# Moving POOL's power for the next tile between the second and the third scatter of the merged stage

## The chip, the cores and the metric

The kernel runs on one core of one Trainium2 chip. The metric is the device time of one execution in microseconds, as the median of several runs. Engines: TensorE (PE), VectorE (DVE), ScalarE (ACT), GpSimd (POOL), and SyncE (SP), which issues plain DMAs.

## The reference

The input has 8,192 tokens of 128 features in fp32. Three blocks follow each other, each with a layer norm ahead and a residual add behind: half of a mixture of experts, linear attention, and half of the same mixture of experts again.

```python
x = x + 0.5 * ffn(layernorm(x), ...)      # mixture of experts
x = x + attention(layernorm(x), ...)      # 32 sequences of 256 tokens, 16 heads of 8
x = x + 0.5 * ffn(layernorm(x), ...)      # mixture of experts, same weights

# ffn: a shared expert for every token, and 2 of 8 routed experts, inner size 256
shared = (silu(x @ shared_gate.T) * (x @ shared_up.T)) @ shared_down.T
probs = sigmoid(x @ router_w.T + routing_bias)
scores, indices = top_k(probs, 2);  scores = scores / sum(scores)
combined = sum over the two picks of score * expert(x)
return shared + combined

# attention: phi = silu + 1, no softmax
kv = phi(k)^T v per head;  out = phi(q) kv;  return out @ Wo.T + bo
```

## The kernel before

Tokens are handled in 16 tiles of 512 (four sub-tiles of 128). There are four stages.

1. **Dispatch** (`f = 0`): each tile is normalised, routed and run through the shared expert. POOL scatters its rows (input, two weights, two addresses) by indirect DMA into regions of DRAM by expert, `first_rows`.
2. **Slots** (`f = 0`): 78 slots of 256 rows go through the routed experts, once for the first picks and once for the second. POOL scatters the results.
3. **Merged stage** (366 to 592 us in the profile): attention and the dispatch of the second mixture of experts run interleaved, one tile of each per turn. In turn `i` attention works on tile `i`, the projections of tile `i + 1`, the transposes and the routing of tile `i - 1` (`LAG_T = 1`) and the shared expert of tile `i - 2` (`LAG_G = 2`).
4. **Slots** (`f = 1`), and the output.

Each engine has its own list of instructions, written out by hand in the order of its turns; the engines meet at semaphores only. An engine that waits holds up everything behind it in its list.

What matters for the change are the steps of the merged stage that hand work from one engine to another, by the tile that they belong to:

- VectorE, turn `i`: `mask_heads(i)` (`kv_sb`), `add_bias(i)`, `value(i + 1, 0)` (`v_sb`), in turns 0 to 8 a late pick (`add_pick`, `x<-xT_lo,x`), the second half of the routing of tile `i - 2` (`place` and four short steps), `multiply(.., 0)` (`h`), `low` (`xT_lo`), `value(i + 1, 1)`, statistics for the late pick or, in later turns, three steps of `first_table`, `add_attention(i)`, `norm_stats` and `variance` (`var`) of tile `i`, the first 13 routing steps of tile `i - 1` (each some 0.22 us from start to start, the last writes `mask`), `shift_rows` (`shift`) of tile `i`, in some turns a `normaliser` of ten steps for a group of up to four attention tiles, `multiply(.., 1)` (`h`), three more routing steps and the reciprocal, `add_shared`.
- POOL, tile `t = i - 2` in turn `i`: `row_numbers`, `pick_weights` (it waits for `place` of its tile; five instructions that end with the write of the weights into `send`), four indirect scatters, and then `deviation`, which is the power: it takes the -0.5th power of `var` of tile `t + 2` and writes `rstd`.
- ScalarE: `send_normalised(1, i)` (`send`) needs `shift` and `rstd` of tile `i`; `high` (`xT_hi`) copies the transposed tile, and VectorE's `low` needs that copy.
- TensorE: the gate and up products of the shared expert (`g_bank`, `u_bank`, lines 1015 to 1017) in two halves, `times_wo` (L1271), transposes (L1037), projections (L1248, L1254), `attend` (L1280), `router` (L1058, it needs `xT_lo`), `down_shared` (L1101), `key_value` (L1264), `ranks` (L1070). The first half of the gate products of a turn needs VectorE's second `h` of the turn before.

`variance(q)` raises `norm_step`, for which `deviation(q)` waits; `deviation` raises `rstd_done`, for which `shift_rows` waits. The power of tile 1 stands ahead of POOL's tile loop, those of tiles 2 to 15 inside it. `norm_step` and `rstd_done` count in the same order before and after.

Of the kernel before, what the change touches and what calls it, by code (L numbers as in the profile page):

```python
# [42 lines left out]
FFN, ATTN = "ffn", "attention"  # L43
LAG_T, LAG_G = 1, 2
# [22 lines left out]
NORM_OF = {item: (q, i) for q, items in enumerate(NORMS) for i, item in enumerate(items)}  # L67
# [7 lines left out]
LOGITS_READ, MASK_STEP, SAFE_STEP, RECIP_STEP, RANKS_READ = 2, 13, 16, 17, 19  # L75
PLACES_STEP = 20
NORM_STEPS, POWER_STEPS = 10, 2
POWER_AFTER = 4
NORM_AHEAD = {4: NORM_OF[(FFN, 0, 8)][0], 8: NORM_OF[(FFN, 0, 12)][0]}
POWERS = list(NORM_AHEAD.values()) + [NORM_OF[(FFN, 1, t)][0] for t in range(NEWTON, TILES)]  # L80
STEPS_OF = [POWER_STEPS if q in POWERS else NORM_STEPS for q in range(len(NORMS))]
# [36 lines left out]
def macaron(nc, x_in, w_experts, router_wT, routing_bias, w_attn, bq, bv, bo, out):  # L118
    tokens = x_in.shape[0]
    tiles = TILES  # L120
# [18 lines left out]
    with ExitStack() as ctx:  # L139
# [217 lines left out]
        def ring_of(f, t):  # L357
            return (f * tiles + t) % SEND_RING
# [37 lines left out]
        def batch_no(f, b):  # L396
            return f * len(BATCHES[0]) + b
# [221 lines left out]
        def _(pool):  # L619
# [36 lines left out]
            def deviation(q):  # L656
                n = len(NORMS[q]) * SUB
                pool.wait_ge(norm_step, STEPS_BEFORE[q] + 1)
                for kind, f, s in NORMS[q - 2]:
                    if kind == FFN:  # L660
                        pool.wait_ge(send_xn_done, f * tiles + s + 1)
                pool.tensor_tensor(rstd[q % 2][:, 0:n], var[:, 0:n], neg_half[:, 0:n], ALU.pow).then_inc(rstd_done, 1)  # L662

            def row_numbers(f, t):
                if f == 0 and t == 0:
                    pool.wait_ge(numbers_ready, 1)
                wait_count(pool, sent[ring_of(f, t)], sent_count(f, t - SEND_RING))
                pool.tensor_copy(send[ring_of(f, t)][:, :, NUMBER].bitcast(I32), number[:, t * SUB:(t + 1) * SUB]
                                 ).then_inc(row_numbered, 1)

            def ffn_tile(f, t):
                b = BATCH_OF[f][t]
                i = t - BATCHES[f][b][0]
                row_numbers(f, t)
                if f == 1:
                    pick_weights(t)
                    pool.wait_ge(weights_step, WEIGHT_STEPS * (t + 1))
                pool.wait_ge(route_step, (batch_no(f, b) + 1) * ROUTE_STEPS)
                pool.wait_ge(row_numbered, f * tiles + t + 1)
                pool.wait_ge(send_xn_done, f * tiles + t + 1)  # L680
                for j in range(SUB):
                    k = i * SUB + j
                    pool.indirect_dma_start(  # L683
                        first_rows, bass.IndirectOffsetOnAxis(ap=send_to[b % SEND_TO_RING][:, k:k + 1], axis=0),
                        send[ring_of(f, t)][:, j, :], None).then_inc(sent[ring_of(f, t)], 16)
                if f == 1 and t + LAG_G < tiles:
                    deviation(NORM_OF[(FFN, 1, t + LAG_G)][0])

            def pick_weights(t):
                n = SUB  # L690
                picks = [a[:, :, 0:n] for a in (score_silu, score_recip, prob)]
                pool.wait_ge(score_silu_done, batch_no(1, t) + 1)
                pool.wait_ge(route_step, batch_no(1, t) * ROUTE_STEPS + RECIP_STEP + 1)
                pool.tensor_tensor(picks[2], picks[0], picks[1], ALU.mult).then_inc(weights_step, 1)
                pool.wait_ge(weights_step, WEIGHT_STEPS * t + 1)
                pool.tensor_tensor(total[:, 0:n], prob[:, 0, 0:n], prob[:, 1, 0:n], ALU.add).then_inc(weights_step, 1)
                pool.wait_ge(weights_step, WEIGHT_STEPS * t + 2)
                pool.tensor_scalar(total[:, 0:n], total[:, 0:n], 2.0, None, ALU.mult).then_inc(weights_step, 1)
                pool.wait_ge(weights_step, WEIGHT_STEPS * t + 3)
                pool.tensor_tensor(inv_total[:, 0:n], total[:, 0:n], minus_one[:], ALU.pow).then_inc(weights_step, 1)  # L700
                pool.wait_ge(weights_step, WEIGHT_STEPS * t + 4)
                wait_count(pool, sent[ring_of(1, t)], sent_count(1, t - SEND_RING))
                pool.tensor_tensor(send[ring_of(1, t)][:, :, WEIGHT:WEIGHT + PICKS].rearrange("p s w -> p w s"), picks[2],
                                   inv_total[:, 0:n].unsqueeze(1).to_broadcast([P, PICKS, n]), ALU.mult).then_inc(weights_step, 1)
# [16 lines left out]
            def dispatch():  # L721
                f = 0
                ffn_tile(f, 0)
                ffn_tile(f, 1)
                split_low(1)
                ffn_tile(f, 2)
                ffn_tile(f, 3)
                split_low(2)
                split_low(3)
                for ts in BATCHES[f][WRITTEN_OUT:]:  # L730
                    for t in ts:
                        ffn_tile(f, t)
                        q = NORM_AHEAD.get(t)
                        if q is not None:
                            deviation(q)
                    for t in ts:
                        if 1 <= t < EXPERTS:
                            split_low(t)
# [1383 lines left out]
```

## Time and profile before

| | us |
|---|---|
| median of 3 runs | 810.29 |
| lowest, highest | 806.66, 812.32 |
| profiled execution, its own time | 810.85 |
| its span | 809.1 |
| TensorE busy | 704.3 (87%) |
| VectorE busy | 553.4 (68%) |
| ScalarE busy | 461.8 (57%) |
| POOL busy | 485.5 (60%) |

Shares of busy time are means over stages that have different limits. TensorE's granted clock was 0.938 of full speed over the span. The time of the execution is 1.75 us longer than the span: what lies around the first and the last recorded instruction.

### The profile page before, as it was taken

Reading aid. Unit: us, or ns where it says so; the run is one execution under the profiler, and the core shown is the slowest. Engines: PE = TensorE matmul, PEld = TensorE weight load, DVE = VectorE, ACT = ScalarE, POOL = GpSimd, SP = SyncE. Lnnn points to the kernel's source line nnn. Section 1 sums busy time; section 2 is a strip of 40 time slices with the busy share of each in tenths; the row PEclk is TensorE's granted clock in tenths of the full one; section 3 lists DMA queues with packets and bytes.
Section 4 is the critical chain, followed back from the end, with each engine's and each line's share of the span. In section 5 each row is a group of like instructions: output and inputs, shape, how many; then the busy total and the mean of one; then the engine's idle time right before and its main releaser. Section 6 shows DMA issues by size and latency. Waiting matters only on the chain.

```text
span 809.1 us, 18241 instructions
## 1 busy us (share of the span) xinstructions
PE 704.3 (87%) x5229; PEld 652.7 (81%) x5229; DVE 553.4 (68%) x1730; ACT 461.8 (57%) x849; POOL 485.5 (60%) x580
## 2 busy tenths in 40 slices
PE   5578849979999899998888989998779999899990
PEld 4466748869999899996677778887679999899990
DVE  6688697875455556787887877787675555455673
ACT  2334525347667657767665657754247667657760
POOL 5253655647777677773354454555537777667773
PEclk7589989989999999999899999999799999999996
DMA  9111163127787475641120000000326788466676
GB/s 279 60 46 45 57 178 89 54 82 207 213 235 242 138 209 169 192 125 34 40 60 21 15 28 15 28 21 22 88 68 192 207 237 233 158 190 180 187 233 230
DMA packets 87956, 103.27 MB, mean 128 GB/s; under 512 B 12212, under 2 KB 70452, under 8 KB 87860
## 3 DMA queue, kind: packets, MB, share of 16 engines
q1 hardware_dynamic: 72244, 64.97, 30.1%
q0 software_dynamic: 15616, 37.14, 12.8%
q8 instruction: 46, 0.75, 0.4%
q14 instruction: 50, 0.41, 0.2%
HBM read 51.57 MB, written 50.49 MB: 126 GB/s over the span
## 4 chain that ended last, share of the span: by engine, by line
PE 42%; POOL 18%; DVE 13%; issue 9%; DMA 3%; ACT 3%; SPq 1%; POOLq 0%; DVEq 0%; ACTq 0%
PE y_bank L1207 11%; POOL first_rows L683 6%; POOL second_rows L712 6%; PE g_bank L1015 4%; PE g_bank L1017 3%; PE g_bank L1016 3%; PE u_bank L1015 3%; PE u_bank L1016 3%; PE u_bank L1017 3%; PE y_bank L1101 3%; DMA row_ring<-second_rows 2%; POOL rstd L662 2%; POOL inv_total L700 2%; DVE h L1439 2%; PE route_bank L1161 1%
## 5 line engine op out<-in xcount | busy, mean ns | idle before, releaser
L1877 DVE TENSOR_TENSOR h<-silu_g,u_bank 128x512 f32<-128x512 f32 x144 | 99.0, 688 | 145.1 <-ACT silu_g L894 138.8
L712 POOL DMA_INDIRECT second_rows<-row_ring x144 | 138.9, 965 | 65.1 <-issue 41.7
L683 POOL DMA_INDIRECT first_rows<-send,send_to x128 | 126.4, 988 | 85.8 <-DVE send L1540 41.6
L712 POOL DMA_INDIRECT y_rows<-row_ring x144 | 141.9, 986 | 58.2 <-issue 32.7
L869 ACT ACTIVATE slot_gu<-w_gu 128x1024 fp32r x132 | 139.8, 1059 | 42.4 <-issue 42.2
L1207 PE MATMUL y_bank<-w_dn,h 128*128 x1152 | 153.1, 276 | 0.2 <-DVE h L1877 0.2
L1207 PEld LDWEIGHTS y_bank<-w_dn,h 128*128 128x128 f32 x1152 | 141.3, 192 | 0.9 <-issue 0.4
L1015 PE MATMUL g_bank<-xT_hi,slot_gu 128*128 128x256 f32 x264 | 86.5, 328 | 12.8 <-DVE xT_lo L1868 12.7
L894 ACT ACTIVATE silu_g<-g_bank 128x512 f32<-128x512 f32 x144 | 83.8, 582 | 15.5 <-PE g_bank L1017 15.3
L1101 PEld LDWEIGHTS y_bank<-w_dn,h 128*128 128x128 f32 x512 | 66.1, 204 | 17.8 <-issue 15.7
L1101 PE MATMUL y_bank<-w_dn,h 128*128 128x128 f32 x512 | 67.3, 288 | 13.5 <-DVE x L1444 13.5
L797 ACT ACTIVATE send<-x,shift,rstd 128x128 f32<-128x128 f32 x128 | 52.2, 482 | 44.6 <-DVE shift L1422 37.1
L1016 PE MATMUL u_bank<-xT_lo,slot_gu 128*128 128x256 f32 x264 | 75.1, 285 | 0.0
L1017 PE MATMUL g_bank<-xT_hi,slot_gu 128*128 128x256 f32 x264 | 75.1, 284 | 0.0
L1017 PE MATMUL u_bank<-xT_hi,slot_gu 128*128 128x256 f32 x264 | 74.9, 284 | 0.0
L1016 PE MATMUL g_bank<-xT_lo,slot_gu 128*128 128x256 f32 x264 | 74.9, 284 | 0.0
L1015 PE MATMUL u_bank<-xT_hi,slot_gu 128*128 128x256 f32 x264 | 74.9, 284 | 0.0
L788 ACT ACTIVATE silu_g<-g_bank 128x512 f32<-128x512 f32 x64 | 38.1, 595 | 60.2 <-PE u_bank L1017 60.0
L1015 PEld LDWEIGHTS g_bank<-xT_hi,slot_gu 128*128 128x128 f32 x264 | 50.6, 192 | 15.0 <-DVE xT_lo L1868 14.6
L1016 PEld LDWEIGHTS g_bank<-xT_lo,slot_gu 128*128 128x128 f32 x264 | 50.9, 193 | 0.0
L1016 PEld LDWEIGHTS u_bank<-xT_lo,slot_gu 128*128 128x128 f32 x264 | 50.5, 191 | 0.0
L1017 PEld LDWEIGHTS g_bank<-xT_hi,slot_gu 128*128 128x128 f32 x264 | 50.5, 191 | 0.0
(257 smaller groups left out, 1638.2 us busy)
## 6 DMA issues: line engine op xcount, KB each, us to landing
row_ring<-second_rows SPq DMA_DIRECT2D x66, 258.0 KB
row_ring<-first_rows SPq DMA_DIRECT2D x66, 132.0 KB
w_raw<-w_experts SPq DMA_DIRECT2D x21, 256.0 KB, 2.8
second_rows<-pad SPq DMA_DIRECT2D x16, 258.0 KB
x<-x_in SPq DMA_DIRECT2D x16, 256.0 KB, 7.1
xT_hi<-y_rows SPq DMA_DIRECT2D x16, 256.0 KB
xT_lo<-y_rows SPq DMA_DIRECT2D x16, 256.0 KB, 2.9
out<-x SPq DMA_DIRECT2D x16, 256.0 KB
```

The costliest lines, as they stand in the source:

```text
L683: pool.indirect_dma_start(first_rows, bass.IndirectOffsetOnAxis(ap=send_to[b % SEND_TO_RING][:, k:k + 1], axis=0), send[ring_of(f, t)][:, ...
L712: pool.indirect_dma_start(to, bass.IndirectOffsetOnAxis(ap=rows[k][:, j, at:at + 1].bitcast(I32), axis=0), rows[k][:, j, columns], None).t ...
L788: act.activation(silu_g[c][:], g_bank[gate_bank(n, c)][:], ACT.Silu).then_inc(silu_done, 1)
L797: last = act.activation(send[ring_of(f, t)][:, j, INPUT:RESULT], x_sub(t, j), ACT.Identity, bias=bias, scale=scale)
L869: act.activation(slot_gu[n % 2][:].rearrange("p a n -> p (a n)"), w_gu[:, bass.ds(e, 1)].rearrange("p e a n -> p (e a n)").bitcast(F32), A ...
L894: act.activation(silu_g[n % 2][:], g_bank[n % 2][:], ACT.Silu).then_inc(slot_silu_done, 1)
L1015: pe.matmul(bank_ap, w_parts[0], x_parts[0], start=True, stop=False)
L1016: pe.matmul(bank_ap, w_parts[0], x_parts[1], start=False, stop=False)
L1017: return pe.matmul(bank_ap, w_parts[1], x_parts[0], start=False, stop=True)
L1101: last = pe.matmul(shared_bank[:, s], h[t % 2][c][:, s], w_dn[:, 0, c, :], start=(c == 0), stop=(c == HALVES - 1))
L1207: last = pe.matmul(y_bank[par][:, j * P:(j + 1) * P], h[par][0][:, c * ROWS + j * P:c * ROWS + (j + 1) * P], w_dn[:, bass.ds(e[j % len(e)] ...
L1877: dve.tensor_tensor(h[par][0][:], silu_g[par][:], u_bank[par][:], ALU.mult).then_inc(slot_h_done, 1)
```

## The change

The call of `deviation` for tile `t + LAG_G` moves from behind the loop over the four scatters into it, behind the second scatter. Its arguments, its waits and its semaphore stay the same, and so do all other engines' lists. The constant `POWER_AFTER` is not used by the kernel before. Tiles 14 and 15 have no such call.

```diff
-POWER_AFTER = 4
+POWER_AFTER = 2
...
                 for j in range(SUB):
                     k = i * SUB + j
                     pool.indirect_dma_start(
                         first_rows, bass.IndirectOffsetOnAxis(ap=send_to[b % SEND_TO_RING][:, k:k + 1], axis=0),
                         send[ring_of(f, t)][:, j, :], None).then_inc(sent[ring_of(f, t)], 16)
-                if f == 1 and t + LAG_G < tiles:
-                    deviation(NORM_OF[(FFN, 1, t + LAG_G)][0])
+                    if f == 1 and j + 1 == POWER_AFTER and t + LAG_G < tiles:
+                        deviation(NORM_OF[(FFN, 1, t + LAG_G)][0])
```

## Rows read from the trace of the kernel before

**Rows 1.** Waits from 366 to 592 us: waiter, releaser, total, times, longest.

```profile
DVE shift L1422 <- POOL rstd L662: 21.3, 14, 2.2
```

**Rows 2.** Timeline of POOL in turn 10: start, us, operation, idle before it.

```profile
518.82 0.96 POOL L683 DMA_INDIRECT first_rows<-send,send_to  x1 [0.30 <-issue]
...
521.34 0.95 POOL L683 DMA_INDIRECT first_rows<-send,send_to  x1 [0.30 <-issue]
522.31 1.06 POOL L662 TENSOR_TENSOR rstd<-var,neg_half 128x4 f32<-128x4 f32 x1
...
526.99 0.20 POOL L694 TENSOR_TENSOR prob<-score_silu,score_recip 128x8 f32<-128x8 f32 x1 [3.48 <-DVE place L1518]
```

**Rows 3.** Timeline of DVE in the same turn.

```profile
514.23 0.22 DVE L1518 TENSOR_TENSOR place<-route_bank,filled 128x64 f32<-128x64 f32 x1
...
518.83 0.18 DVE L1414 TENSOR_SCALAR var<-stats 128x4 f32<-128x4 f32 x1
...
521.61 0.19 DVE L1500 TENSOR_TENSOR mask<-best,first_best 128x32 bf16<-128x32 f32 x1
523.40 0.16 DVE L1422 SCALAR_TENSOR_TENSOR shift<-stats,rstd 128x4 f32<-128x4 f32 x1 [1.60 <-POOL rstd L662]
```

**Rows 4.** Timeline of PE in the same turn.

```profile
511.83 0.50 PE L1015 MATMUL g_bank<-xT_hi,w_gu 128*128 128x512 f32 x1 [0.24 <-DVE h L1439]
...
515.29 1.05 PE L1280 MATMUL y_bank<-kvo_sb,phi_q 128*128 128x128 f32 x8
516.47 0.28 PE L1058 MATMUL route_bank<-router_parts,xT_hi 128*128 128x16 f32 x1
...
521.51 1.06 PE L1264 MATMUL y_bank<-phi_k,v_sb 128*128 128x128 f32 x8
522.40 0.60 PE L1037 MATMUL tr_bank<-ident,xn 128*128 128x128 f32 x4
...
524.22 0.50 PE L1015 MATMUL g_bank<-xT_hi,w_gu 128*128 128x512 f32 x1 [0.23 <-DVE h L1439]
```

**Rows 5.** Windows, power to power: PE, PEld, DVE, ACT, POOL busy; PE clock; DMA.

```profile
442.83:455.86 13.03, 12.06 (x82) 10.17 (x81) 10.72 (x38) 8.56 (x19) 7.08 (x11) 1.00 0.06 22
...
481.88:497.52 15.64, 13.43 (x82) 11.52 (x81) 11.21 (x45) 9.97 (x23) 7.06 (x11) 0.89 0.06 19
...
509.93:522.31 12.38, 12.01 (x82) 10.12 (x81) 10.04 (x38) 8.56 (x19) 7.06 (x11) 1.00 0.07 23
...
547.13:559.54 12.41, 11.60 (x78) 9.71 (x77) 10.17 (x38) 6.65 (x14) 7.06 (x11) 1.00 0.07 24
559.54:571.63 12.09, 8.91 (x65) 7.26 (x63) 9.36 (x36) 3.93 (x9) 7.12 (x12) 1.00 0.07 22
```

**Rows 6.** Timeline of DVE: shift behind the powers of four other turns.

```profile
414.05 0.16 DVE L1422 SCALAR_TENSOR_TENSOR shift<-stats,rstd 128x4 f32<-128x4 f32 x1 [1.59 <-POOL rstd L662]
...
427.66 0.16 DVE L1422 SCALAR_TENSOR_TENSOR shift<-stats,rstd 128x4 f32<-128x4 f32 x1 [0.95 <-POOL rstd L662]
...
560.62 0.16 DVE L1422 SCALAR_TENSOR_TENSOR shift<-stats,rstd 128x4 f32<-128x4 f32 x1 [1.48 <-POOL rstd L662]
...
572.71 0.16 DVE L1422 SCALAR_TENSOR_TENSOR shift<-stats,rstd 128x4 f32<-128x4 f32 x1 [1.98 <-POOL rstd L662]
```

**Rows 7.** Timeline of all engines round the first power in the tile loop.

```profile
398.40 1.06 POOL L662 TENSOR_TENSOR rstd<-var,neg_half 128x4 f32<-128x4 f32 x1
...
398.69 0.19 DVE L1500 TENSOR_TENSOR mask<-best,first_best 128x32 bf16<-128x32 f32 x1
...
399.49 0.16 DVE L1422 SCALAR_TENSOR_TENSOR shift<-stats,rstd 128x4 f32<-128x4 f32 x1 [0.61 <-POOL rstd L662]
```

**Rows 8.** Timeline of all engines, turn with a normaliser for four tiles.

```profile
482.96 0.16 DVE L1422 SCALAR_TENSOR_TENSOR shift<-stats,rstd 128x4 f32<-128x4 f32 x1 [1.61 <-POOL rstd L662]
...
485.12 1.65 ACT L781 ACTIVATE xn<-x,attn_shift,attn_rstd 128x128 f32<-128x128 f32 x4 [5.06 <-DVE attn_shift L1406]
...
491.67 0.28 PE L1058 MATMUL route_bank<-router_parts,xT_hi 128*128 128x16 f32 x1
```

## The prediction

> **What bounds the kernel now.** I began with the table of waits over the merged stage (366 to 592 us) and looked for VectorE behind the operation that moves. VectorE's `shift` waited 14 times for POOL's power, 21.3 us together [rows 1]. The reader should ask whether this wait ends last, so next comes one turn on three engines. On POOL the scatters of a tile follow each other at 1.26 us, the power starts 0.02 us behind the end of the fourth (522.29) and ends at 523.37; then POOL is idle 3.48 us until the next tile's `place` [rows 2]. On VectorE `var`, which the power reads, is there at 519.01, the last mask of the routing ends at 521.80, and `shift` starts at 523.40: 1.60 us idle [rows 3]. Behind `shift` stand `h`, the bias, `v_sb` and the next `place`, and `place` starts POOL's next chain. So today's loop is place, POOL's weights, four scatters, power, shift, place. From `place` at 514.23 to the end of the power it takes 9.14 us.
>
> TensorE must be read with care. It is shown busy 12.01 of 12.38 us in a turn without a late pick, and 12.06 of 13.03 in one with it [rows 5]: the same work in more time. Its ends are modelled, so part of a wait is hidden in busy time. In the turn of [rows 4] it waits 0.24 us for `h` at 511.83. From the attention product (515.29) to the router (516.47) it takes 1.18 us, while eight matmuls of the same form elsewhere in the turn, from 521.51 to 522.40, take 0.89: another 0.29 us, spent waiting for `xT_lo`. TensorE's own turn is then 524.22 - 511.83 = 12.39, less 0.53: about 11.85 us.
>
> **The change part by part.** Nothing is added or removed; 14 powers move ahead of the third and fourth scatter of their tile. The power of the merged stage that stands before the tile loop does not move (it is the one I leave out: POOL waited for `var` there, not VectorE for POOL).
>
> *The power earlier.* The second scatter ends at 518.82 + 0.96 = 519.78, and `var` is ready at 519.01, 0.77 us before. The power ends at about 519.80 + 1.06 = 520.86, while VectorE reaches `shift` at 521.80. The wait is gone, with 0.94 us to spare. Should the power start 0.30 us behind a scatter, as the next scatter does [rows 2], it still hides. Bounds of what the move takes off VectorE in this turn: 1.60 us (all) and 0.
>
> *Two scatters later.* Scatters three and four end 1.06 us later, or 1.36 with another 0.30 us gap, by 523.65. POOL's row numbers (0.18) follow and POOL is then idle for over 3 us [rows 2]. The cover is 3.48 us long now; with a turn 0.55 us shorter and POOL free at 523.65 + 0.18, some 2.6 us of it are left (526.99 - 0.55 - 523.83). What reads those rows is a load far behind the tile's own turn. The `send` buffers are used again after six tiles. Cost 0. Without the cover it would be 0.3 us a tile.
>
> *The new wait of POOL.* If `var` came late, scatters three and four would wait behind it. It has 0.77 us in hand, and if the whole of `var`'s delay beyond that were real, the power would still end no later than it does now, so no loss can come from this side while `place` keeps its lead. I take 0; for each us by which `var` came later than that, scatters three and four would lose one, out of the 2.6 us of cover.
>
> *What is late next.* VectorE's own turn is 12.39 - 1.60 = 10.8 us here, and 13.03 - 1.6 = 11.4 with a late pick. TensorE needs 11.85 in both. So TensorE becomes the bound, and the saving is not the wait: **0.55 us in a turn of 12.39 and 1.17 in one of 13.03**. I count from one gate product on TensorE to the next:
> - Tile 0 (wait 0.61 us [rows 7]): 0. TensorE and ScalarE are behind there at half clock, and `h` would wait for `silu_g` instead.
> - Tiles 1 and 2 (1.59 and 0.95 [rows 6]): these turns carry two late picks, four extra statistics and the normaliser for four tiles, and VectorE bounds them: 2.5 us.
> - The turn behind them (ends at 444.7) is held by ScalarE's chain, then by TensorE: 0.2.
> - Two turns of 13.03: 2 x 1.17 = 2.3.
> - The pair from 470.8 to 499.4, one window like the first of [rows 5] and the one of 15.64 us there, 28.7 together. A normaliser of four tiles stands behind the shift. In the new frame, with the gate product at 0, the router starts at 516.47 - 511.83 - 0.29 = 4.35 and the mask ends 5.33 us later (521.80 - 516.47), at 9.7. From shift to `xn` takes 485.12 - 482.96 = 2.16, from `xn` to the router 491.67 - 485.12 = 6.55 [rows 8], and from router to the next gate product 11.85 - 4.35 = 7.5. Sum 25.9; saved 2.8.
> - Three turns of 12.39: 3 x 0.55 = 1.65, taken as 1.7.
> - The last three turns. In the first the transposes of the attention input are gone, TensorE is busy 0.41 us less (11.60 against 12.01 [rows 5]), bound 11.45, saved 1.0. In the other two TensorE has less still (8.91 us in the last window [rows 5]) and VectorE bounds: their waits of 1.48 and 1.98 [rows 6] go whole, 3.5.
>
> Sum: 2.5 + 0.2 + 2.3 + 2.8 + 1.7 + 4.5 = **14.0 us** of 21.3. The expert slots behind start that much sooner and are otherwise the same.
>
> *A rule against the change.* Until now VectorE stood idle for most of each power; now it routes beside it. In [rows 7] a power ran from 398.40 to 399.46 beside a mask step with two operands in SBUF: 0.19 us, as in [rows 3]. I count no contention. The Trainium skill, "SBUF — State Buffer", section "SBUF: two separate sides", says that a VectorE instruction with two SBUF inputs and a GpSimd instruction that reads SBUF lock each other out of a shared port for a whole instruction. By that rule the routing would stand still during the power; the row speaks against it, one case as it is. The second rival below is that case.
>
> **How the numbers follow.** The profiled execution took 810.85 us, 809.1 of them span. 810.85 - 14.0 = 796.9. It stands 0.56 us above the median of 810.29, so I forecast **796.3 us**. Runs of before lie between 806.66 and 812.32; about 1% (8 us) is what a measurement of this kernel can tell from no change.
>
> - **TensorE becomes the bound** (forecast): 0.60. Own range 793 to 800, from 0.2 us per turn either way in the 11.85.
> - **VectorE keeps all of its wait.** If the 11.85 is too long because the modelled matmuls hide more waiting, the whole 21.3 less the 0.61 of tile 0 comes back: 789.6. For it: the turn at 481.88 had its clock at 0.89 [rows 5], and fewer gaps may spare that. Against it: TensorE's matmuls start without a gap in the rest of the turn. Chance 0.10.
> - **Power and routing exclude each other.** VectorE stands still 1.06 us of the 1.60 it wins, its turns become 11.9 and 12.5 us, and each of 13 powers gives 0.54: 7 us, 803.3. The same figure stands for any latency that I took as covered (`xT_lo` has only some 0.1 us behind ScalarE's `xT_hi` in the new frame). Chance 0.17.
> - **The change does not do what it says**: the power would be held until the scatters' descriptors are finished, so that its end stays where it was. The gap of 0.02 us behind the fourth scatter [rows 2] speaks against it. 810. Chance 0.06.
> - **Slower: TensorE's clock.** It was granted at 1.00 (2.4 GHz) in the steady turns and 0.89 on average, so partly at 1.2 GHz, in the turn with the long gap [rows 5]. New, short waits in another place of each turn could bring it down each time. In the turn of 15.64 us TensorE's busy time is 1.4 us over the 12.01 of a steady one [rows 5]. At that price the gain of 14.0 is used up when 10 of 13 turns fall; in all 13 it costs 18 us, so 814.5. The steady turns hold 1.00 with gaps of 0.24 and more in TensorE, which speaks against it. Chance 0.03.
> - The remaining 0.04 is spread on either side.
>
> The range from the second case to the third, 789.5 to 803.5, leaves out about 0.15. Faster by over 1% (below 802.2) holds the first two, a third of the third and half of the remainder: 0.80. Within 1%: 0.17. Slower: 0.03.
>
> **What the changed profile would show.** The power stands between scatters two and three and ends about 1 us before `shift`; the row `shift` waits for `rstd` is gone or below 1 us in all; scatters three and four end about 1.1 to 1.4 us later against `place`; steady windows are 11.8 to 11.9 us with and without a late pick alike; VectorE now waits for ScalarE's `xT_hi` or `silu_g`, some 0.5 to 1 us a turn; mask steps keep 0.19 us. The forecast is wrong if turns with and without a pick still differ by 0.6 us (VectorE bounds, second rival or third), if the routing steps are stretched beside the power, or if the clock of a steady window falls below 1.00.

## The result and the profile after

| | before | after |
|---|---|---|
| median, us | 811.25 (4 runs) | 788.89 (4 runs) |
| lowest to highest, us | 806.66 to 812.32 | 786.57 to 789.84 |
| span of the profiled execution, us | 809.1 | 788.1 |

The ratio is 0.9731, with a 95% interval from 0.9686 to 0.9775: 2.7% faster, 22.4 us between the medians, 21.0 us between the spans. I had forecast 14.0 us and 796.3 us in all; the time lies 0.6 us under the range.

The page of the changed kernel: the span, each engine's busy time and the granted clock of TensorE in 40 slices.

```profile
span 788.1 us, 18241 instructions
...
PE 691.0 (88%) x5229; PEld 644.4 (82%) x5229; DVE 554.2 (70%) x1730; ACT 460.1 (58%) x849; POOL 486.5 (62%) x580
...
PEclk8588898989999999999999999999989999999995
```

The waits of the merged stage after the change (columns as in [rows 1]). The row of `shift` behind the power, 21.3 us before, is gone. POOL itself now waits for `var`: 9.6 of the 10.5 us belong to the power ahead of the tile loop, 0.33 and 0.54 to two tiles.

```profile
POOL rstd L662 <- DVE var L1414: 10.5, 3, 9.6
```

POOL and VectorE of the changed kernel in the turn of [rows 2] and [rows 3].

```profile
505.55 1.11 POOL L683 DMA_INDIRECT first_rows<-send,send_to  x1 [0.60 <-POOL send L703]
506.96 0.96 POOL L683 DMA_INDIRECT first_rows<-send,send_to  x1 [0.30 <-issue]
507.95 1.05 POOL L662 TENSOR_TENSOR rstd<-var,neg_half 128x4 f32<-128x4 f32 x1
509.19 1.03 POOL L683 DMA_INDIRECT first_rows<-send,send_to  x1 [0.20 <-issue]
```

```profile
502.38 0.21 DVE L1518 TENSOR_TENSOR place<-route_bank,filled 128x64 f32<-128x64 f32 x1
...
504.18 0.69 DVE L1433 TENSOR_TENSOR xT_lo<-tr_bank,xT_hi 128x512 fp32r<-128x512 f32 x1 [0.19 <-ACT xT_hi L770]
...
507.33 0.17 DVE L1414 TENSOR_SCALAR var<-stats 128x4 f32<-128x4 f32 x1
...
508.07 0.19 DVE L1493 TENSOR_TENSOR best<-z,score 128x32 f32<-128x32 f32 x1
508.30 0.19 DVE L1496 TENSOR_TENSOR best<-best,counting 128x32 f32<-128x32 f32 x1
...
510.10 0.19 DVE L1500 TENSOR_TENSOR mask<-best,first_best 128x32 bf16<-128x32 f32 x1
510.21 0.15 DVE L1422 SCALAR_TENSOR_TENSOR shift<-stats,rstd 128x4 f32<-128x4 f32 x1
```

The power starts 0.03 us behind the second scatter and ends at 509.00. The last mask step ends at 510.29 and `shift` starts at 510.21, with no wait. VectorE does wait for ScalarE's `xT_hi` (0.19 us): it has run ahead of the others. `shift` now starts 2.17 us ahead of the next first gate product (512.38), before the change 0.82 (523.40 and 524.22). Routing steps beside the power, at 508.07 and 508.30, read two operands in SBUF each and keep 0.19 us and a distance of 0.23. Behind the power the third scatter starts after 0.19 us and lasts 1.03 us instead of 0.96, and POOL's copy behind the fourth starts 4.54 us after the second scatter, before the change 4.52. The three windows below, again from power to power with the columns of [rows 5], are a turn with a late pick, one with the normaliser for four tiles, and one without a late pick.

```profile
437.33:448.71 11.38, 11.38 (x81) 10.08 (x80) 10.68 (x38) 8.46 (x20) 7.20 (x12) 1.00 0.07 24
...
471.42:485.54 14.12, 12.28 (x81) 10.23 (x80) 11.80 (x49) 8.38 (x20) 7.18 (x11) 1.00 0.07 21
...
496.54:507.95 11.41, 11.41 (x81) 10.10 (x80) 10.39 (x41) 8.57 (x20) 7.18 (x12) 1.00 0.08 25
```

Turns with and without a pick now have the same length, 11.4 us, and TensorE's busy time is the whole window. This is what the forecast said of the bound, at another size. One of its signs missed: it wanted VectorE to wait 0.5 to 1 us a turn. In the three turns without a pick VectorE waits 1.3 us together, and in the two with one it doesn't wait at all, so there its list is as full as TensorE's.

TensorE in the same turn of the changed kernel, then those lines of the kernel before that [rows 4] left out.

```profile
500.98 0.49 PE L1015 MATMUL g_bank<-xT_hi,w_gu 128*128 128x512 f32 x1
...
502.24 0.39 PE L1017 MATMUL u_bank<-xT_hi,w_gu 128*128 128x512 f32 x1
502.47 0.60 PE L1271 MATMUL y_bank<-attn_raw,kv_sb 128*128 128x128 f32 x4
502.91 0.60 PE L1037 MATMUL tr_bank<-ident,send 128*128 128x128 f32 x4
...
504.21 1.05 PE L1280 MATMUL y_bank<-kvo_sb,phi_q 128*128 128x128 f32 x8
505.02 0.26 PE L1058 MATMUL route_bank<-router_parts,xT_hi 128*128 128x16 f32 x1
...
512.27 0.25 PE L1072 MATMUL route_bank<-mask,all_ones 128*128 128x64 bf16 x4
512.38 0.49 PE L1015 MATMUL g_bank<-xT_hi,w_gu 128*128 128x512 f32 x1
```

```profile
513.09 0.39 PE L1017 MATMUL u_bank<-xT_hi,w_gu 128*128 128x512 f32 x1
513.44 0.71 PE L1271 MATMUL y_bank<-attn_raw,kv_sb 128*128 128x128 f32 x4
513.99 0.60 PE L1037 MATMUL tr_bank<-ident,send 128*128 128x128 f32 x4
...
523.74 0.25 PE L1072 MATMUL route_bank<-mask,all_ones 128*128 128x64 bf16 x4
```

The reader should compare starts with starts, not busy times. `u_bank` to `kv_sb`'s product: 0.35 us before, 0.23 after. That product to the transposes: 0.55 and 0.44. `attend` to the router: 1.18 and 0.81 (with its first step 0.03 more). Ranks to the next gate product: 0.48 and 0.11. Together 0.12 + 0.11 + 0.37 + 0.03 + 0.37 = 1.00 us, and the turn went from 12.39 to 11.40. I had found 0.53 of it.

From gate product to gate product (`g_bank`, L1015, the first half of each turn) the time divides so:

| stretch (times of the kernel before) | before | after | saved | forecast |
|---|---|---|---|---|
| 386.6 to 430.5: tiles 0, 1, 2 | 43.9 | 40.5 | 3.4 | 2.5 |
| to 444.7: the turn behind | 14.3 | 13.9 | 0.4 | 0.2 |
| to 470.8: two turns with a late pick | 26.0 | 22.8 | 3.3 | 2.3 |
| to 499.4: the pair with the normaliser | 28.7 | 25.5 | 3.2 | 2.8 |
| to 536.6: three turns without a pick | 37.2 | 34.2 | 3.0 | 1.7 |
| to 573.5: the last three with a power | 36.9 | 31.1 | 5.8 | 4.5 |
| to 595.4: last tiles, table, first slot | 21.9 | 18.3 | 3.6 | 0 |

The rows sum to 22.7; the first gate product came 0.4 us later and the slots behind took 214.9 us instead of 213.7, which leaves the 21.0 of the spans.

Two parts of this sum can't be laid to the change on these traces. One is the last row, which is taken up with the runs below. The other is 1.6 us of the first row, the turn of tile 0. It took 15.80 us before (386.59 to 402.39) and 14.17 after (386.99 to 401.16), with TensorE busy for 13.21 and 11.59 us at a granted clock of 0.78 and 0.88. TensorE's distances from start to start show half speed from about 394.0 to 400.9 us before, and from 395.0 to 398.4 after. The two spells differ before the first moved power starts (396.58), and the second one ends before that power's `shift` (399.19), so the trace shows no way from the change to this gain. The clock of this turn was 0.87 or 0.88 in seven of the runs below, among them router_before and bias_before, where the power keeps its old place and length; it was 0.78 in last2, p3 and twice_after and 1.00 in router_after and norm_early. Why is open. Without these two parts 17.4 us remain, for which the forecast had 14.0.

### The profile page after: what moved, and what is told of

It is laid out like the page before. It is cut to its first block, busy times and chain, and to the rows that moved or that the text cites. A ratio compares the mean times of both kernels' runs of the same rounds, so it can differ in the third digit from the quotient of the medians.

```text
span 788.1 us, 18241 instructions
## 1 busy us (share of the span) xinstructions
PE 691.0 (88%) x5229; PEld 644.4 (82%) x5229; DVE 554.2 (70%) x1730; ACT 460.1 (58%) x849; POOL 486.5 (62%) x580
## 4 chain that ended last, share of the span: by engine, by line
PE 50%; DVE 18%; POOL 7%; issue 7%; DMA 4%; ACT 3%; SPq 1%; POOLq 0%; ACTq 0%; DVEq 0%
PE y_bank L1207 11%; POOL second_rows L712 6%; PE g_bank L1015 4%; PE y_bank L1101 4%; PE g_bank L1016 4%; PE g_bank L1017 4%; PE u_bank L1015 4%; PE u_bank L1016 4%; PE u_bank L1017 4%; DMA row_ring<-second_rows 2%; DVE h L1439 2%; PE route_bank L1161 1%; PE tr_bank L1161 1%; DVE stats L1366 1%; PE u_bank L1192 1%
## 5 line engine op out<-in xcount | busy, mean ns | idle before, releaser
L1015 PE MATMUL g_bank<-xT_hi,slot_gu 128*128 128x256 f32 x264 | 86.3, 327 | 13.4 <-DVE xT_lo L1868 13.0
L894 ACT ACTIVATE silu_g<-g_bank 128x512 f32<-128x512 f32 x144 | 83.6, 581 | 15.7 <-PE g_bank L1017 15.6
L1015 PE MATMUL u_bank<-xT_hi,slot_gu 128*128 128x256 f32 x264 | 74.8, 283 | 0.0
L1015 PEld LDWEIGHTS g_bank<-xT_hi,slot_gu 128*128 128x128 f32 x264 | 50.4, 191 | 15.7 <-DVE xT_lo L1868 14.9
L1015 PEld LDWEIGHTS u_bank<-xT_hi,slot_gu 128*128 128x128 f32 x264 | 50.3, 191 | 0.0
```

Of the source, the lines that this page charges most:

```text
L894: act.activation(silu_g[n % 2][:], g_bank[n % 2][:], ACT.Silu).then_inc(slot_silu_done, 1)
L1015: pe.matmul(bank_ap, w_parts[0], x_parts[0], start=True, stop=False)
```

## The experiments

All are set against runs of the kernel before on the same chip. Each was profiled once.

**Where the power stands.** The constant alone changes, to 1 and to 3.

```diff
-POWER_AFTER = 2
+POWER_AFTER = 1
```

> The power stands behind the first scatter instead of the second. Theory (with the power behind the second scatter VectorE has time in hand at the shift, and TensorE sets the steady turns at 11.39 us): nothing is left to win. 789 us, within 3 us of the changed kernel; POOL now waits some 0.5 us a tile for var. Rival (VectorE or the power is still in the loop of the turns): the power 0.7 us earlier in 13 turns gives another 9 us, 780.

788.79 us, ratio 0.975 (0.9719 to 0.9781): as the changed kernel, and each steady turn stays at 11.38 to 11.40 us. An earlier power is worth nothing.

```diff
-POWER_AFTER = 2
+POWER_AFTER = 3
```

> The power stands behind the third scatter. Theory: in the changed kernel shift starts 7.8 us behind place, and a power behind the third scatter would end 7.9 us behind place, so only some 0.1 us a turn comes back: 788 to 791 us. Rival (every step of the power's place counts, as it would if POOL's chain still bounded the turns): 1.26 us in each of 13 turns, 805.

794.41 us, ratio 0.9808 (0.9777 to 0.9838). Neither value: 5.5 us over the changed kernel, more than the 0 to 2 that I expected and far from the rival's 16. Its trace says where. Turns without a pick stay at 11.39 us, those with one grow to 11.87, and the last two lose their lead: 1.0 us in the two turns with a pick, 0.9 in the pair, 1.2 in the last three. Another 1.6 us lie in the turns of tiles 0 to 2 and 1.3 in the stretch to the first slot, the two parts whose cause is open. The timeline of one turn of it, all engines:

```profile
505.23 0.21 DVE L1518 TENSOR_TENSOR place<-route_bank,filled 128x64 f32<-128x64 f32 x1
...
512.06 1.05 POOL L662 TENSOR_TENSOR rstd<-var,neg_half 128x4 f32<-128x4 f32 x1
...
513.14 0.16 DVE L1422 SCALAR_TENSOR_TENSOR shift<-stats,rstd 128x4 f32<-128x4 f32 x1
```

The power ends at 513.11, 7.9 us behind `place`, and `shift` follows it at once; in a turn with a pick, where VectorE reaches `shift` sooner after `place`, that is a wait again. So the path is near critical behind the third scatter and clear behind the second.

**The power doubled.** A second one of the same size stands ahead of the real one.

```diff
+                if NORMS[q][0][1] == 1:
+                    pool.tensor_tensor(spare[:, 0:n], neg_half[:, 0:n], neg_half[:, 0:n], ALU.pow)
                 pool.tensor_tensor(rstd[q % 2][:, 0:n], var[:, 0:n], neg_half[:, 0:n], ALU.pow).then_inc(rstd_done, 1)
```

> The changed kernel, with each power behind the second scatter doubled: one more power of the same size into a spare tile goes just ahead of the real one. rstd then ends some 7.7 us behind place instead of 6.6. In the changed kernel the shift starts 7.8 us behind place in a short turn and about 7.5 in one with a late pick. Theory (the power has time in hand): 0 in the short turns, about 0.3 us in each long one as with the power behind the third scatter; 791 to 794 us. Rival (the power still counts in full): 1.04 x 14 = 15 us, 804.

787.44 us (786.84 to 793.06), ratio 0.9719 (0.9693 to 0.9745); its profiled span was 791.3. In the trace turns without a pick keep 11.39 us and those with one take 11.6, 0.2 more, about as expected; the median lies below the 791 to 794 that I expected and within the spread of the changed kernel's runs. Some 15 us of added work on POOL cost at most 3.2, by the spans.

**The same path shortened without moving anything.** In the kernel before, a copy stands where the power stood, so that `rstd` holds the variance itself; the routing of the second mixture of experts then works on other values.

```diff
+                if NORMS[q][0][1] == 1:
+                    pool.tensor_copy(rstd[q % 2][:, 0:n], var[:, 0:n]).then_inc(rstd_done, 1)
+                    return
                 pool.tensor_tensor(rstd[q % 2][:, 0:n], var[:, 0:n], neg_half[:, 0:n], ALU.pow).then_inc(rstd_done, 1)
```

> The kernel before, with the power at its old place, but in the merged stage a copy of var stands in its place: rstd of the second mixture of experts is wrong by that, its shape and the amount of work are the same. A copy of this size takes POOL 0.18 us instead of 1.06. Theory (what cost time was the length of the path place, weights, four scatters, power, shift, whatever the order on POOL): 0.87 us less in each turn that VectorE's wait sets, 13 x 0.87 = 11 us plus up to 3 us of half clock behind the last turns, 797 to 800 us. Rival (the change gained by what follows the scatters, or by a gentler order of POOL's descriptors): no gain from this, 811.

794.69 us, ratio 0.9811 (0.9786 to 0.9836): 15 us less. A turn without a pick, gate product to gate product:

```profile
491.60 0.48 PE L1018 MATMUL g_bank<-xT_hi,w_gu 128*128 128x512 f32 x1
...
503.13 0.47 PE L1018 MATMUL g_bank<-xT_hi,w_gu 128*128 128x512 f32 x1
```

That is 11.53 us, 0.87 less than 12.40; turns with a pick took 12.14, 0.87 less than 13.01. The dose is met exactly in the steady turns, so it was the length of the path behind `place` that counted, with the order of the scatters untouched. The total beats my 797 to 800 by what lies outside the steady turns: the turn of tile 0 took 14.2 us instead of 15.8 and had a clock of 0.88, and the slots behind, whose values have changed, took 212.2 instead of 213.7.

**Which engine is the bound.** Four router matmuls on `xT_lo` are left out in the merged stage, 0.44 us of TensorE a turn, after the change and before it.

```diff
-                    pe.matmul(logits, hi[:, s], router_parts[:], start=True, stop=False)
-                    last = pe.matmul(logits, lo[:, s], router_parts[:], start=False, stop=True)
+                    last = pe.matmul(logits, hi[:, s], router_parts[:], start=True, stop=(f == 1))
+                    if f == 0:
+                        last = pe.matmul(logits, lo[:, s], router_parts[:], start=False, stop=True)
```

> The changed kernel, with the four router matmuls on xT_lo left out in the merged stage, so the second routing is coarser. TensorE has 4 x 0.11 = 0.44 us less work a turn. Theory (TensorE sets the turns without a late pick at 11.39 us and VectorE's own work stands at 10.8 there, and at 11.4 in the turns with a late pick): the turns without a pick shrink by about 0.4 us, those with one by 0.1 at most; 787 us in all. Rival (VectorE still sets them all): every turn keeps its length, 789.

787.43 us, ratio 0.9736 (0.9701 to 0.9771). The total alone couldn't tell this from 789. The turns can: one with a late pick, then one without.

```profile
439.01 0.48 PE L1015 MATMUL g_bank<-xT_hi,w_gu 128*128 128x512 f32 x1
...
450.39 0.48 PE L1015 MATMUL g_bank<-xT_hi,w_gu 128*128 128x512 f32 x1
```

```profile
509.17 0.47 PE L1015 MATMUL g_bank<-xT_hi,w_gu 128*128 128x512 f32 x1
...
520.11 0.47 PE L1015 MATMUL g_bank<-xT_hi,w_gu 128*128 128x512 f32 x1
```

11.38 us in the first, as in the changed kernel, and 10.94 in the second, 0.45 less than 11.39; the other turn with a pick took 11.35, the other two without one 10.94 and 11.00. Without a pick TensorE alone was the bound; with one, VectorE's list of the same length takes over: by my sum it is 13.01 - 1.62 = 11.39 us, and in the two turns of this run VectorE waits for nothing, while TensorE now waits 0.34 us for its `xT_lo`.

> The kernel before, with the same four router matmuls on xT_lo left out in the merged stage. Theory (before the change VectorE and POOL set the turns and TensorE waits 1.0 us in each): turns keep 12.40 and 13.02 us, 809 us in all, 2 us less at most from the first and last turns. Rival (TensorE's modelled busy time of 97% was right and it was the bound already): 0.44 us in each of some 12 turns, 804.

808.31 us, ratio 0.9979 (0.9957 to 1.0001). The same turn as in [rows 4]:

```profile
509.34 0.51 PE L1015 MATMUL g_bank<-xT_hi,w_gu 128*128 128x512 f32 x1 [0.69 <-DVE h L1440]
...
521.74 0.50 PE L1015 MATMUL g_bank<-xT_hi,w_gu 128*128 128x512 f32 x1 [0.69 <-DVE h L1440]
```

12.40 us, not a hundredth less: the 0.44 us taken from TensorE came back as a longer wait for `h`, 0.69 instead of 0.24. The rival, that TensorE was the bound already at a busy share of 97%, falls.

Now VectorE: attention's output bias goes to 8 columns of one sub-tile instead of the whole tile.

```diff
-                dve.tensor_tensor(by_sub(x_tile(t)), by_sub(x_tile(t)), bo_b[:].unsqueeze(1).to_broadcast([P, SUB, P]), ALU.add
-                                  ).then_inc(bias_added, 1)
+                dve.tensor_tensor(x_sub(t, 0)[:, 0:8], x_sub(t, 0)[:, 0:8], bo_b[:, 0:8], ALU.add).then_inc(bias_added, 1)
```

> The changed kernel, with the output bias of attention added to 8 columns of one sub-tile only instead of all 512 elements a partition: VectorE has about 0.45 us less work a turn. Theory (TensorE is the bound of the steady turns): they keep 11.39 us, gains only in the few turns with a normaliser, 787 to 789 us. Rival (VectorE is the bound): 0.45 us in each of 14 turns, 783.

788.00 us, ratio 0.971 (0.9679 to 0.9741). Steady turns kept 11.38 to 11.40 us, with a late pick and without. With a pick the two engines are equally long, so neither run alone shortens those turns by more than 0.03 us; no run takes work off both.

> The kernel before with the same bias on 8 columns only. Theory (before the change VectorE's list is in the loop: shift, h, bias, place): 0.45 us less in each of 14 turns, 811 - 6 = 805 us. Rival (TensorE already was the bound, so that VectorE has time to spare): 811. Beside the run on the changed kernel this shows whether the bound moved from one engine to the other.

805.90 us, ratio 0.994 (0.9917 to 0.9964). A turn without a pick took 12.15 us instead of 12.40:

```profile
497.40 0.50 PE L1015 MATMUL g_bank<-xT_hi,w_gu 128*128 128x512 f32 x1 [0.23 <-DVE h L1439]
...
509.55 0.50 PE L1015 MATMUL g_bank<-xT_hi,w_gu 128*128 128x512 f32 x1 [0.24 <-DVE h L1439]
```

I had expected 0.45 us a turn and got 0.25, in both kinds of turn. VectorE's next instruction behind the bias shows why:

```profile
511.36 0.42 DVE L1929 TENSOR_TENSOR v_sb<-g_bank,bv_b 128x256 f32<-128x256 f32 x1 [0.18 <-ACT phi_k L924]
```

It starts 0.34 us behind the start of the bias (511.02) instead of 0.60 (513.30 to 513.90 in the kernel before), and 0.18 of the 0.34 is a new wait for ScalarE. Without that wait the gain would have been 0.44. The direction is clear: VectorE's work counted before the change and does not after it.

**One part of the change alone.** The powers issued with tiles 12 and 13, then the counterpart, then tiles 0 to 2 (edits to the changed kernel).

```diff
-                    if f == 1 and j + 1 == POWER_AFTER and t + LAG_G < tiles:
+                    if f == 1 and j + 1 == (POWER_AFTER if t < 12 else SUB) and t + LAG_G < tiles:
```

> As the changed kernel, but the powers issued with tiles 12 and 13 stay behind the fourth scatter. Theory (the last two powers were worth their VectorE waits of 1.48 and 1.98 us and also a spell of TensorE at half clock behind them, some 3.6 us): 789 + 7 = 796 us, with the last routed tile's gate products at 0.43 us from start to start again. Rival (the clock had nothing to do with these powers): 789 + 3.5 = 792.5.

796.28 us, ratio 0.9806 (0.9759 to 0.9852). TensorE behind the last power in this kernel, then in the changed one:

```profile
558.99 0.50 PE L1015 MATMUL g_bank<-xT_hi,w_gu 128*128 128x512 f32 x1 [2.45 <-DVE h L1439]
...
565.16 0.77 PE L1015 MATMUL g_bank<-xT_hi,w_gu 128*128 128x512 f32 x1
565.73 0.63 PE L1016 MATMUL g_bank<-xT_lo,w_gu 128*128 128x512 f32 x1
...
567.87 3.04 PE L1101 MATMUL y_bank<-w_dn,h 128*128 128x128 f32 x16
```

```profile
554.91 0.50 PE L1015 MATMUL g_bank<-xT_hi,w_gu 128*128 128x512 f32 x1 [0.38 <-DVE h L1439]
...
559.49 0.48 PE L1015 MATMUL g_bank<-xT_hi,w_gu 128*128 128x512 f32 x1
559.81 0.40 PE L1016 MATMUL g_bank<-xT_lo,w_gu 128*128 128x512 f32 x1
...
560.99 1.27 PE L1101 MATMUL y_bank<-w_dn,h 128*128 128x128 f32 x10
```

From 565.16 to 567.87 gate products follow each other at 0.43 us, half speed (in the window from 560 to 566 us the granted clock was 0.50, that is 1.2 GHz); in the changed kernel they keep 0.23 us and a window from 553 to 560 us shows 1.00. TensorE had waited 2.45 us ahead of the slow spell, and 0.38 in the changed kernel. By time alone the rival isn't out, for the interval reaches from 791.3 to 798.8 us; the trace shows that the spell was there, and the next two runs bear on whether it belongs to the wait.

```diff
-                    if f == 1 and j + 1 == POWER_AFTER and t + LAG_G < tiles:
+                    if f == 1 and j + 1 == (POWER_AFTER if t >= 12 else SUB) and t + LAG_G < tiles:
```

> As the kernel before, but the powers issued with tiles 12 and 13 move behind the second scatter. Theory, the counterpart of the run before: 3.5 us of waits and 3.6 us of half clock go: 811 - 7 = 804 us. Rival (only the waits): 807.5. If the two parts do not add up to the whole change, the savings of the early turns and the late ones depend on each other.

804.14 us, ratio 0.993 (0.9903 to 0.9957): 6.7 us for two of 14 powers. The first12 kernel saved 14.6; together 21.3, so the parts add up within their intervals. Yet the split is not what I expected: the stretch from the last gate product to the first slot fell from 21.9 to 19.5 us here, not to 18.3.

```diff
-                    if f == 1 and j + 1 == POWER_AFTER and t + LAG_G < tiles:
+                    if f == 1 and j + 1 == (POWER_AFTER if t < 3 else SUB) and t + LAG_G < tiles:
```

> As the kernel before, but only the powers issued with tiles 0, 1 and 2 move. My own sum gave 2.5 us for them and nothing for tile 0: 808. The trace of the changed kernel shows 3.4 us up to the gate product behind tile 2, and 0.4 in the turn behind it: by that 807. Rival (the early gain hangs on the later moves): 811.

805.25 us, ratio 0.9954 (0.9936 to 0.9973): 4.1 us, near the 3.8 of the changed kernel's trace and more than my 2.5. Its own trace has 3.5 us in the turns of tiles 0 to 2, of which 1.6 in that of tile 0, and nothing in the turn behind. And here, with the full wait of 2.45 us ahead of it, the stretch to the first slot took 19.5 us. So that stretch is not settled by the wait ahead of it. Over all traces it took 21.9, 21.9, 21.0, 21.0, 20.5 and 19.5 us behind a wait of 1.6 to 2.5 us, and 19.5, 19.5, 19.5, 19.1 and four times 18.2 to 18.3 behind one of 1.2 or less. A shorter wait goes with a faster stretch, by 2.1 us between the means of the two groups, but with one trace of each kernel the share of the change in the 3.6 us stays open. What the length itself goes by is TensorE's clock: the stretch had a mean granted clock of 0.76 to 0.77 in the two traces of 21.9 us, 0.83 in the three of 20.5 to 21.0, 0.89 to 0.91 in the five of 19.1 to 19.5, and 0.95 to 0.98 in the four of 18.2 to 18.3.

**A version beyond both.** The attention normaliser of a group moves ahead of the statistics of the expert norm (and the list of norm calls with it).

```diff
-        calls.append([(FFN, 1, t)])
-        calls += [items for items in groups if LATE_TURN.get(items[-1][2]) == t]
+        late = [items for items in groups if LATE_TURN.get(items[-1][2]) == t]
+        calls += late + [[(FFN, 1, t)]] if t >= LAG_G else [[(FFN, 1, t)]] + late
...
                         add_attention(i)
+                        norm_late(i)
                         norm_stats((FFN, 1, i))
                         variance(NORM_OF[(FFN, 1, i)][0])
...
                         shift_rows(NORM_OF[(FFN, 1, i)][0])
-                    norm_late(i)
```

> The changed kernel, with the attention normaliser of a group moved in VectorE's list from behind shift to a place between add_attention and the statistics of the expert norm, so that ScalarE gets attn_shift some 3 us sooner in the turns with a group (4, 5, 6, 7 and 8 hold late tiles; groups of four end in two of them). Theory (in these two turns of 15.35 and 14.12 us ScalarE's chain xn, send, pad, phi_k sets the pace now, and the power has 2 us of cover to give up): 1.5 to 3.5 us less, 785.5 to 787.5. Rival (the later statistics and var hold POOL and TensorE's down product as long as they save ScalarE): no change or 1 to 2 us more, 789 to 791.

785.18 us, ratio 0.9696 (0.967 to 0.9722). Interval and that of the changed kernel overlap, but the traces agree on the place: from gate product to gate product the pair took 24.1 us instead of 25.5, and the two turns round the first group 25.8 instead of 27.4. These 2.9 us are the better part of the 5.1 between the spans; another 1.1 lie in the turn of tile 0, which ran at a clock of 1.00. The median is just below the 785.5 to 787.5 that I expected. ScalarE and `shift` in the turn with a group, changed kernel first:

```profile
473.39 0.15 DVE L1422 SCALAR_TENSOR_TENSOR shift<-stats,rstd 128x4 f32<-128x4 f32 x1
...
475.66 1.65 ACT L781 ACTIVATE xn<-x,attn_shift,attn_rstd 128x128 f32<-128x128 f32 x4 [3.47 <-DVE attn_shift L1406]
...
477.22 1.63 ACT L797 ACTIVATE send<-x,shift,rstd 128x128 f32<-128x128 f32 x4
```

```profile
469.98 1.64 ACT L781 ACTIVATE xn<-x,attn_shift,attn_rstd 128x128 f32<-128x128 f32 x4
...
473.29 0.17 DVE L1422 SCALAR_TENSOR_TENSOR shift<-stats,rstd 128x4 f32<-128x4 f32 x1
...
473.49 1.65 ACT L797 ACTIVATE send<-x,shift,rstd 128x128 f32<-128x128 f32 x4 [1.88 <-DVE shift L1422]
```

`xn` used to follow `shift` by 2.3 us and now precedes it by 3.3; `send` follows `shift` at once. By its median it is the fastest kernel of the study.

## Why the forecast of 14.0 us was too small

**The mechanism held.** The wait for the power is gone, the power's `var` was there in time, the two later scatters cost nothing, and TensorE took over as the bound at one length for both kinds of turn (with a pick, VectorE's list is just as long). The router and bias runs, each on both kernels, show the bound on either side of the change, and the copy in place of the power shows what it was before.

**The step that failed is the size of "TensorE's own turn".** I wrote: 12.39 us, less 0.53, about 11.85. It is 11.39. I had looked for hidden waits at two boundaries and taken them as all; there were four, and at those two I was short by 0.11 and 0.13 us. The `kv_sb` boundary, 0.12 + 0.11 us, I had not priced at all. At `attend` I had taken the 0.89 us from the same eight matmuls to the transposes as the unhindered distance; before the router it is 0.81. My own range allowed 0.2 us a turn. The error of 0.46 us stands in each turn that TensorE bounds: 1.0 in the two turns with a pick, 1.3 in the three without, 0.4 in the pair, and 0.5 in the first of the last three.

**"The last three turns" had a second mistake.** I gave the last two their own waits. The middle one of the three saved 2.2 us (12.40 to 10.15) where I had 1.48: in the TensorE-bound turns VectorE had gained a lead that it could spend as soon as TensorE's work fell. In the first12 kernel, where the power stood late again, that lead shortened its first late turn from 12.40 to 11.70 us and the next kept 12.09.

**Tiles 0 to 2** gave 3.4 us for 2.5, and differently divided: 1.6 in the turn of tile 0, which I had set at nothing and whose gain is the clock's, and 1.8 in the next two, where I had 2.5. So the waits there were over-sized. The run with these three alone has 3.5 us in its trace, so the early saving does not depend on the rest.

**"The expert slots behind start that much sooner and are otherwise the same"** left out the stretch between and so put it at nothing, without a reason. It fell by 3.6 us in the trace, the largest single error of the sum. TensorE spent less of it at 1.2 GHz (busy 11.7 us instead of 15.7, granted clock 0.98 instead of 0.77); how much belongs to the change is open, as said. The traces thus have 8.6 us more than the 14.0: 3.6 here, 3.2 in TensorE's own turn, 0.8 in the last two turns, 0.9 in tiles 0 to 2 and 0.2 in the turn behind, less rounding.

**The rivals.** "VectorE keeps all of its wait" named 789.6 us, nearly the result, and is still wrong as a cause: by it the turns would be 10.8 and 11.4 us long, and they are both 11.4. Its number came out by luck, through TensorE's smaller floor, the clock in the turn of tile 0 and the stretch to the first slot. That power and routing exclude each other falls with the routing steps' unchanged 0.19 us and with `shift`'s missing wait; the rule of the Trainium skill ("SBUF — State Buffer", "SBUF: two separate sides") that stood behind it did not show at these sizes, 4 elements a partition beside 32. That the power would be held to its old end falls with its row at 507.95. The clock stayed at 1.00 in every steady turn. The rival in which the gain moves with POOL's order rather than with the path falls with the copy run.

The low end of the range was that rival's price, which counts at most the waits of `shift` themselves and nothing for the stretch behind. Of its 20.7 us the turns gave 17.4, tile 0 left out; the 1.6 us of tile 0 and the 3.6 of the stretch carried the time below it. (The chances for more than 1% faster add up to 0.78, not 0.80; nothing hangs on it.)

## What to carry to other kernels

When the next bound is an engine whose ends are modelled, find its own turn from starts alone: compare each gap between two of its operations with the same gap where nothing can hold it, at every boundary where another engine hands something over. A wait in the middle of a loop through three engines costs its full length only until the next engine is full; a run that takes work off that engine, on the kernel before and on the one after, tells which of the two you have. Read the turns, not the total: a rival gave the right total here with turns that did not exist.

## What the runs showed of the hardware

- POOL, 1.06 us of power directly between two scatters: the next scatter starts 0.19 us after the power, against 0.30 us after a scatter, and takes 1.03 us instead of 0.96. Moving it cost POOL nothing.
- TensorE's busy share in a turn was 97% (12.01 of 12.38 us) while it waited 1.00 of 12.39 us. The share says little of the room that is left.
- A slow spell of TensorE (0.43 us from start to start instead of 0.23) followed a wait of 2.45 us in the first12 kernel (granted clock 0.76 over the stretch of 21.9 us), and behind the same wait in the first3 kernel it was shorter (0.89 over 19.5 us). In the turn of tile 0 such a spell lasted 6.9 us in the trace of before and 3.4 in that of after, and the two differ from their start, which lies ahead of the first moved power.
- The stretch of the second expert slots took 212.6 to 214.9 us in the nine traces in which neither it nor its values were changed: some 0.15% of the whole on each side. With the runs that change values (router, bias, copy) it is 211.0 to 215.6.
